# Two attention stages, the pairs of experts around them and the next recurrence step written in one interleaved order

## The reference

```python
def _L0_ffn_ref(x, gate_w, gate_b, w1, b1, w2, b2, gamma, beta):      # E = 16 experts, K = 2
    topk_vals, topk_idx = jax.lax.top_k(x @ gate_w + gate_b, K)
    topk_w = jax.nn.softmax(topk_vals, axis=-1)
    h = jax.nn.relu(jnp.einsum('bsh,ehf->bsef', x, w1) + b1)
    expert_out = jnp.einsum('bsef,efh->bseh', h, w2) + b2
    sel = jnp.take_along_axis(expert_out, topk_idx[:, :, :, None], axis=2)
    moe = jnp.sum(topk_w[..., None] * sel, axis=2)
    ...                                                                # layer norm of x + moe

def _L1_attn_ref(x, Wq, bq, Wk, bk, Wv, bv, Wu, bu):
    ...
    scores = jnp.einsum('bihe,bjhe->bhij', q, k) / jnp.sqrt(e)
    scores = jnp.where(j >= i, -jnp.inf, scores)                       # strictly causal
    att = jax.nn.softmax(scores, axis=-1)
    out = jnp.einsum('bhij,bjhe->bihe', att, v).reshape(b, t, h * e)
    return out @ Wu + bu

def step(carry, xs):                                                   # the recurrence, scanned over T
    h, c = carry
    i_t = sigmoid(xi_t + h @ V_i); g_t = tanh(xg_t + h @ V_c); o_t = sigmoid(xo_t + h @ V_o)
    c_new = h * c + i_t * g_t
    return (o_t * tanh(c_new), c_new), o_t * tanh(c_new)
```

## Time and profile before

| stage | us from the start | PE busy | granted clock |
|---|---|---|---|
| state-space mixer, gates | 0 to 241 | | |
| pairs 0 to 47 | 241 to 351 | all of 262 to 346 | 1.00 |
| first attention, with its borders | 346 to 410 | 48.8 of 64 | 0.92 |
| pairs 48 to 95, 32 steps of the recurrence | 410 to 547 | 131.8 of 137 | 0.99 |
| second attention | 547 to 726 | 156.2 of 179 | 0.90 |
| 64 steps of the recurrence alone | 726 to 866 | 95.8 of 140 | 0.51 |

### The profile page before, as it was taken

The page is one execution under the profiler, slowest core; times in us unless marked ns, Lnnn a source line. Parts: engine busy times, 40 slices in busy tenths (PEclk is TensorE's granted clock), DMA queues, the critical chain, the costliest instruction groups (busy, mean ns, idle before and its releaser), DMA issues.

```text
span 865.8 us, 16453 instructions
## 1 busy us (share of the span) xinstructions
PE 702.4 (81%) x6414; PEld 416.6 (48%) x6414; DVE 533.9 (62%) x1104; ACT 360.0 (42%) x667; POOL 252.1 (29%) x223
## 2 busy tenths in 40 slices
PE   4687887853689999787989999788899887776775
PEld 3674654543522222253334442366477665555554
DVE  4856577569684655374886766268667673556443
ACT  2232444423334555444445555425555434232332
POOL 4248575549100314020430304025223230011000
PEclk9999788965599999899999999769999978555555
DMA  9730000000063433001222322000000000000000
GB/s 191 139 70 5 2 1 1 1 1 0 7 191 113 139 113 114 2 2 37 89 71 86 97 88 66 5 2 2 2 2 2 2 1 5 7 11 7 11 8 13
DMA packets 42402, 36.85 MB, mean 43 GB/s; under 512 B 20888, under 2 KB 29848, under 8 KB 42328
## 3 DMA queue, kind: packets, MB, share of 16 engines
q1 hardware_dynamic: 41242, 35.57, 15.3%
q10 hardware_dynamic: 1088, 0.26, 0.2%
HBM read 33.85 MB, written 1.97 MB: 41 GB/s over the span
## 4 chain that ended last, share of the span: by engine, by line
PE 58%; DVE 22%; ACT 7%; issue 5%; POOL 3%; DMA 2%; SPq 1%; POOLq 0%; DVEq 0%; ACTq 0%
PE PS L1569 10%; PE PS L1556 10%; PE PS L1532 6%; PE PS L1603 4%; PE PS L1582 3%; PE PS L1651 3%; PE PS L1662 3%; PE PS L1518 2%; DVE XC L925 2%; PE PS L1624 2%; PE PS L1320 2%; PE PS L1635 2%; PE PS L1329 2%; DMA BIG<-in_x 2%; DVE st L907 1%
## 5 line engine op out<-in xcount | busy, mean ns | idle before, releaser
L1569 PE MATMUL PS<-Y,W1f 64*128 64x512 f32 x384 | 109.8, 650 | 4.4 <-DVE Y L1066 2.9
L1556 PE MATMUL PS<-XC,w2s 128*64 128x512 f32 x384 | 104.0, 622 | 0.6 <-ACT XC L709 0.6
L1532 PE MATMUL PS<-LS,V 64*64 64x32 f32 x1140 | 70.9, 270 | 38.5 <-DVE LS L1195 38.5
L709 ACT ACTIVATE XC<-PS 128x1024 f32<-128x1024 f32 x68 | 69.4, 1021 | 59.4 <-PE PS L1556 48.6
L1532 PEld LDWEIGHTS PS<-LS,V 64*64 64x64 f32 x1140 | 58.9, 188 | 71.0 <-DVE LS L1195 64.3
L1066 DVE TENSOR_TENSOR Y<-XD,UF 128x512 f32<-128x512 f32 x96 | 70.2, 743 | 17.0 <-DMA UF<-gd 9.1
L566 POOL TENSOR_TENSOR Y<-XC 128x512 f32<-128x512 f32 x12 | 14.0, 1166 | 173.1 <-DVE XC L1046 173.1
L1182 DVE SCALAR_TENSOR_TENSOR LS<-LS 128x32 f32<-128x32 f32 x96 | 21.8, 227 | 56.6 <-ACT LS L807 43.4
L1556 PEld LDWEIGHTS PS<-XC,w2s 128*64 128x64 f32 x384 | 19.2, 135 | 73.8 <-issue 61.2
L1569 PEld LDWEIGHTS PS<-Y,W1f 64*128 64x128 f32 x384 | 29.5, 187 | 51.5 <-issue 27.9
L178 POOL TENSOR_TENSOR st<-st,mhalf 128x8 f32<-128x8 f32 x24 | 39.3, 1637 | 37.8 <-DVE st L910 37.8
(11 more groups left out here) (236 smaller groups left out, 1474.7 us busy)
## 6 DMA issues: line engine op xcount, KB each, us to landing
UF<-gd SPq DMA_DIRECT2D x192, 128.0 KB, 2.9
BIG<-in_x SPq DMA_DIRECT2D x8, 512.0 KB, 12.0
out<-X SPq DMA_DIRECT2D x48, 32.0 KB, 2.0
W1f<-in_L_ffn_w SPq DMA_DIRECT2D x2, 512.0 KB, 6.3
EX<-in_L_ffn_w SPq DMA_DIRECT2D x1, 1024.0 KB, 15.2
H<-in_txt SPq DMA_DIRECT2D x2, 256.0 KB, 12.2
w2s<-in_L_ffn_w SPq DMA_DIRECT2D x1, 512.0 KB, 9.5
gd<-EX SPq DMA_DIRECT2D x6, 64.0 KB, 1.7
```

Source lines behind the costliest of these rows:

```text
L709: act.activation(Hb[:, b:b + 2, :], PS[:, b:b + 2, :], ACT.Relu).then_inc(S("m_h"), 1)
L1532: mm = pe.matmul(PS[r, b, o:o + HN], V3[r, g, :], HB[r, (t - 1) % 4, :], start=False, stop=True, skip_group_check=True)
L1556: mm = pe.matmul(PS[64 * h:64 * h + 64, 6, :], w2s[:, 2 * p + h, :], Hb[:, n % 2 * 2 + h, :], start=(p == 0), stop=(p == E // 2 - 1))
L1569: mm = pe.matmul(PS[:, n % 2 * 2 + h, :], W1f[r, 2 * p + h, :], Rb[r, n % 4, :], start=True, stop=True)
```

## The change

It writes the borders of the two attentions into the pairs and into the recurrence, and moves tables. `queries` and `u_out` can use banks 4 and 5. Group 0's queries are made in slots 46 and 47, those of groups 4 and 5 in slots 91 to 94 (`EARLY`); group 1's queries and unit 0's and 4's `score` stand among the last `down`s. At the end of `attend0`, pairs 48 and 49 are weighed and their `up`s stand between the last `gather`s; their `down`s follow from slot 50 on. In `attend0` DVE does `keys_out` ahead of `total`, and `total(0)` after `masked(1)`. The last `project` of the second attention moves behind the next recurrence step. The recurrence starts at slot 59, `residual` at 52 and 63; settling of a chunk ends a slot or two earlier, and the last chunk's first three steps stand in slots 91 and 92.

```diff
-        TAIL_DVE = {0: (0, 1), 1: (2, 3, 4, 5), 2: (6, 7), 3: (8, 9), 4: (10,), 5: (11, 12), 6: (13, 14)}
-        TAIL_POOL = {0: ("sq0",), 1: ("pw0", "mu0", "ga"), 3: ("sq1",), 4: ("pw1", "mu1")}
+        TAIL_DVE = {0: (2, 3, 4, 5), 1: (6, 7), 2: (8, 9), 3: (10,), 4: (11, 12), 6: (13, 14)}
+        TAIL_POOL = {0: ("sq0",), 1: ("pw0", "mu0", "ga"), 2: ("sq1",), 4: ("pw1", "mu1")}
+        EARLY = {46: ((0, 0),), 47: ((0, 1),), 91: ((4, 0),), 92: ((4, 1),), 93: ((5, 0),), 94: ((5, 1),)}
-        LS0 = 3 * E + 8
+        LS0 = 3 * E + 11
-        LATER = dict(s0=-5, k0=-4, k1=-4, s1=2, k2=3, k3=3, k4=4, k5=4, sq0=5, k6=6, k7=6, pw0=6, mu0=7, ga=7, k8=9, k9=9, k10=10,
-                     sq1=10, k11=11, k12=11, pw1=11, mu1=12, out=13, t0=14, t1=14, k13=14, k14=15)
-        XB = (3 * E, 3 * E + 8, None, None, NPR + 12, NPR + 28)
+        LATER = dict(s0=-5, k0=-4, k1=-4, s1=2, k2=3, k3=3, k4=4, k5=4, sq0=4, k6=5, k7=5, pw0=5, mu0=6, ga=6, k8=8, k9=8, k10=9,
+                     sq1=9, k11=10, k12=10, pw1=10, mu1=11, out=12, t0=13, t1=13, k13=13, k14=13)
+        XB = (3 * E + 4, 3 * E + 15, None, None, NPR + 12, NPR + 28)
...
+        def gate_pair(k):
+            return (k + 1) % 2          # bank of a step's gates, was k % 2
...
@@ ACT, slots
+                for G, half in EARLY.get(g, ()):
+                    u_out(G, half, 4)
                 if pair_ends(g) and g < NPR:
                     relu(g, 0)
+                    if g == AT[0]:
+                        u_out(1, 0, 4)
+                        u_out(1, 1, 4)
                     product_out(g // (E // 2))
+                if g == LS1:
+                    o_out(len(UNITS) - 1)
@@ DVE, attend0
+                    if x == us[-1] + 2:
+                        dve.wait_ge(S("a_z"), JOBS[us[-1]])
+                        weigh(AT[0] + 1)
+                        weigh(AT[0] + 2)
@@ PE, attend0
+                    if x == us[-1] + 2:
+                        up(AT[0] + 1)
                     if x - 2 in us:
                         gather(x - 2, 0)
+                    if x == us[-1] + 2:
+                        pe.wait_ge(S("pt_ev"), us[-1] + 1)
+                        up(AT[0] + 2)
@@ PE, slots
-                    pe.wait_ge(S("z_ev0"), (JOBS[U] + 1) // 2)
-                    pe.wait_ge(S("z_ev1"), JOBS[U] // 2)
                     pe.wait_ge(S("u_ev0"), 2 * G)
-                    pe.wait_ge(S("o_ev"), G)
+                if g == AT[0] + 3:
+                    pe.wait_ge(S("z_ev0"), (JOBS[units_of(0)[-1] + 1] + 1) // 2)
+                    pe.wait_ge(S("z_ev1"), JOBS[units_of(0)[-1] + 1] // 2)
+                    pe.wait_ge(S("o_ev"), NB // GA)
                 if t:
                     gates_h(t)
...
+                    if t == XS:
+                        project(NG - 1, len(UNITS) - 1, 2 * NG)
-                if g < NPR:
+                if g < NPR and g not in (AT[0] + 1, AT[0] + 2):
                     up(g)
...
+                for G, half in EARLY.get(g, ()):
+                    ...
+                    queries(G, half, 2 * G + half, 0, 0, b=4)
+                if g == AT[0]:
+                    pe.wait_ge(S("m_h"), g)
+                    score(0)
+                    queries(1, 0, 2, 0, 0, b=4)
+                    down(g - 1)
+                    turn_s(0)
+                    queries(1, 1, 3, 0, 0, b=4)
+                    down(g)
+                elif g == AT[1]:
+                    pe.wait_ge(S("m_h"), g)
+                    score(units_of(1)[0])
                     down(g - 1)
                     down(g)
```

More of the change, by code:

```diff
@@ L360, in settling @@
         def settling(g, *parts):
-            return [(j, p) for j in range(NC - 1) for p in parts if SB[j] + LATER[p] == g]
+            return [(j, p) for j in range(NC) for p in parts if SB[j] + LATER[p] == g and (j < NC - 1 or p in ("s0", "k0", "k1"))]
         def residual(g, *parts):
@@ L753, in attend0 @@
             def attend0(us):
-                for half in range(2):
-                    u_out(UNITS[us[0]][1], half)
                 for x in span_of(us):
-                    if x + 1 in us:
+                    if x and x + 1 in us:
                         u_out(x + 1, 0)
@@ L1666, in attend0 @@
             def attend0(us):
-                nU, nO, nX = 0, 0, 0
-                for half in range(2):
-                    queries(0, half, nU, nO, nX)
-                    nU += 1
+                nU, nO, nX = 4, 0, 0
                 for x in span_of(us):
+                    if x == 0:
+                        continue
                     if x in us:
                         score(x)
+                    if x == 1:
+                        pe.wait_ge(S("m_mo"), (AT[0] + 1) // (E // 2))
                     if x + 1 in us:
@@ L1698, in attend @@
             def attend(us):
-                nU, nO, nX = 2 * UNITS[us[0]][1], UNITS[us[0]][1], us[0]
-                for half in range(2):
-                    queries(UNITS[us[0]][1], half, nU, nO, nX)
-                    nU += 1
+                nU, nO, nX = 2 * UNITS[us[0]][1] + 4, UNITS[us[0]][1], us[0]
                 for x in span_of(us):
                     nxt = next_u(x, us) if x in us else ()
-                    if x in us:
+                    if x in us and x != us[0]:
                         score(x)
                     for u in due(x, us, 2):
-                        project(UNITS[u][1], u, nU)
-                        nO += 1
+                        if u != us[-1]:
+                            project(UNITS[u][1], u, nU)
+                            nO += 1
                     if 0 in nxt:
```

58 lines of the change are left out of this document (35 added, 23 removed).

## The result

The changed kernel takes 859.88 us (median of 20 runs, 851.17 to 866.13) against 875.73 us for the kernel before (median of 20 runs beside them). The ratio is 0.9838, 95% interval 0.9809 to 0.9867: 14.2 us faster, 11.6 to 16.7. This ratio and all that follow compare only the faster executions of each kernel, so they are not quite the ratio of the two medians (0.982 here). The gain is more than the measurement is uncertain, and less than 2%: the outcome that the prediction called "the same". My range held the time; my gain of 21.9 us was 8 us too large.

A forecast was written before the change was run, and what follows sets the result against it. PE was the engine to watch; gain could only be filled idle time and kept clock. 7.0 + 1.8 - 0.5 + 10.5 + 3.1 = 21.9 us, from a mean of 870.6 gives 848.7, stated as 848; range 835 to 862.

The forecast's parts named there:

- the same: Whole kernel: outcome of a time within 2% of the kernel before; chance 0.29.
- A: Start of the first attention: filling PE's waits gains 7.0 us, bounds 4 and 8.
- The 0.85: Start of the first attention: 0.85 us taken off the 7.85 gain for clock, because of new idle pieces.
- B: End of the first attention: `up(48)` and `up(49)` fill waits between the last gathers; gain 1.8 us, bounds 0 and 3.
- C: Pairs that carry the recurrence: -0.5 us, bounds -6 and +4; +3 if POOL could take the later operation first.
- The 5.4: Slots 58 to 61: 5.4 us gained as `residual` of chunk 1 no longer meets chunk 2's end of settling.
- the wait in slot 57: Pairs with the recurrence: PE's turn of chunk 0 waits 3.5 us for POOL's in-order operations, 8.3 us from `k7`'s end.
- D: Start of the second attention: 9 us by score(7) plus 1.5 later, gain 10.5 us, bounds 6 and 13.
- a rival: "Slower": slot 57's wait drops the clock, pairs with steps run at half, up to 928 us; chance 0.03.
- POOL and DVE in the moved slots: Pairs with the recurrence: longer slot 57 wait, settled chunks stall steps, -6 there; gain 16, 854 us; chance 0.09.
- E: End of the second attention: first `gates_x` no longer waits for the projection and its copy; gain 3.1 us, bounds 1 and 4.
- two signs of being wrong: Queries in slots 91 to 94 make PE wait for ACT; pairs before the first attention stretch beyond the queries added.

The follow-up runs named there:

- the tables alone: The kernel before with only the new LS0, XB and LATER tables, both attention borders as before; 880.0 us against 873.0, ratio 1.0087.
- after: The changed kernel itself, with the whole change, against the kernel before; 859.88 us against 875.73, ratio 0.9838.

## Why the prediction was right or wrong

**A: right.** Score(1) came 6.04 us earlier (predicted 6.0), score(3) 7.9 (7.85). The 0.85 that I gave back for the clock was not due: the stretch has 1.00.

**B: right.** 1.7 against 1.8, with `up(50)` behind one relu as described.

**C: wrong, by 7 us in this profile.** It is more than the whole error of the sum, because the other four terms together came 2.6 us better than written and hid a part of it. The sum was 5.4 - 3.5 - 2.4. The 5.4 came: none of the waits of the earlier trace rows is left at its place. The working for the wait in slot 57 was sound (`k7` ends 13.3 us after `up(50)`, predicted 13.5; PE is there at 18.4, as predicted; POOL's six operations take 9.0 from there, not 8.3), so 4.1 against 3.5. What failed is the size of the rest:

- I gave no clock to that wait. PE runs at 0.50 behind it: the turn, the `up` and the `down` that follow take 1.05, 2.00 and 1.70 us from one row's start to the next (428.56, 429.61, 431.61, 433.31) where the clock's other level gives 0.59, 1.06 and 1.01: 2.1 us more (my expectations for the experiments say 2.7). I had made the rule myself ("an idle microsecond there costs more than itself"), applied it in A and D, and used it in C only for a rival.
- I took a step behind `k13` and `k14` (1.4) and the slots around chunk 1 (1.0) as 2.4 us together, with nothing for `weigh` or for bank 7. The waits are 3.8 for the steps, 2.2 for the two clashes over bank 7, 1.2 for `weigh`: 7.2. (Before, the steps had 2.1 and `weigh` 0.2; the 2.1 is mostly the wait of 1.71 inside the 5.4.) Of the 3.8, up to 1.7 are the two steps whose DVE operation was held beside POOL, which no term of mine had. The bank clash I had not looked for: `out` and `s0`/`s1` of neighbouring chunks can be read from the tables, as users of one bank in one slot.
- In sum 4.1 + 2.1 + 7.2 = 13.4 us came and 5.4 + 0.2 went, which gives the measured -7.8. This is a sum of pieces that fits to some tenths, not one that was fixed by experiment piece by piece: the experiments took away the wait on POOL and the two clashes.

And -7.8 is the mild side. With these same tables and the same waits, `up(50)` to `up(91)` took 128.4, 128.9, 128.9, 132.6, 132.6 and 132.7 us in six profiles (one of them the tables alone); in the longer ones PE's clock falls once more behind a step's wait of 1.4 us (granted 0.91 and 0.75 in two stretches of 10 us where after has 1.00, with the same 8.6 us of busy time in the first). At 132.6, C would be -11.5 and the gain 13.5 us, near the timed 14.2. Which of the two is the commoner, six single profiles can't tell.

So the outcome was my rival "POOL and DVE in the moved slots", which I had given 0.09 with C at -6, and even its -6 was too kind. POOL took its six operations in their order (`pw0` at 419.49 to `mu` at 427.23), so the wait stood, at 4.11 us, and C was not +3.

**D: right in this profile.** Score(6) came 8.15 us earlier (8.0), score(7) 8.24 (8.3), the idle piece was 4.80 us (4.4), the half clock behind it short (3.68 and then 1.93 for a score; 6.5 us from the start of score(6), where I had said 8). That it was short is partly luck: in two of nine profiles it was not. The later gain was 3.3 us instead of 1.5, and why is open. But I took the price of the half clock as one number, 1.8 us, from one profile. It goes up to 6.8, as shown above, and nearly half of the piece goes when four passes of DVE are moved. (The idle piece of 2 us that I set beside the earlier trace rows is not in that row; the trace has it, 1.99 us ahead of the score at 701.02.)

**E: right in size, 3.85 against 3.1,** and in mechanism: 1.5 from moving the project, and the other 2.3 fit the dropped wait.

**The time.** The range 835 to 862 held 859.9 near its upper end, and its width did that, not the sum. The forecast of 848 missed by 12 us. The gain was 7.7 too large, and the start 5.1 too low, for I counted from a mean of 870.6 us of four executions, and the median of 20 is 875.7. My two signs of being wrong did not show: the first queries in slots 91 to 94 made PE wait 0.3 us for ACT, and `up(47)` came 0.9 us later for 1.06 us of queries put in.

**The chances.** I had 0.67 for faster by over 2%. (The pieces as I list them add up to 0.66, 0.31 and 0.03 rather than 0.67, 0.29 and 0.04.) The evidence against lay in the earlier trace rows: two chunks that need POOL in the same slots, priced at the idle time alone. With the 2.1 us of clock C would have been -2.6, with the bank clash too -4.8; the gain is then 17.6, and the time on the edge of the 2%.
